# A four-layer graph network on one core: the adjacency handed over in three layouts, the transposed tile loaded and double-buffered

## The reference

```python
# layer 0: gated by the neighbours' keys
w = isqrt * mask * einsum('bid,bid->bi', q, einsum('bij,bjd->bid', adj, k * mask))
x += softmax(w, axis=1)[:, :, None] * v
# layer 1: attention weighted by adj, one head
weight = adj * exp(q @ k.T);  weight /= weight.sum(axis=2);  x += weight @ v
# layer 2: eight heads, scores multiplied by adj + adj
x += softmax(q @ k.T * scale * (adj + adj)) @ v @ Wo + bo
# layer 3: three-hop propagation
t = adj * exp(leaky_relu(sj[:, None, :] + si[:, :, None] + ab))
t /= t.sum(-1) + 1e-12
x += relu(h @ Wk[0] + (t @ h) @ Wk[1] + (t @ t @ h) @ Wk[2] + bk.sum(0))
```

## Time and profile before

| | |
|---|---|
| median of 3 runs | 2275.75 us (2275.45 to 2278.11) |
| profiled execution | 2281.91 us, span 2280.1 us |
| TensorE busy | 2246.0 us (99%), granted clock 0.995 |
| VectorE, ScalarE, GpSimd busy | 1314.0, 784.9, 717.8 us |
| DMA | 224.75 MB, 185048 packets, queue of SyncE 35.1% of 16 engines |

### The profile page before, as it was taken

One profiled execution on the slowest core, in us unless ns is written; L12 is line 12 of the kernel. 1 busy time (PEld: TensorE's weight loads), 2 busy tenths in 40 slices (PEclk: granted clock), 3 DMA queues, 4 the chain that ended last, 5 costly groups with the idle time before them and its releaser, 6 DMA issues.

```text
span 2280.1 us, 39533 instructions
## 1 busy us (share of the span) xinstructions
PE 2246.0 (99%) x15903; PEld 1779.9 (78%) x15903; DVE 1314.0 (58%) x2645; ACT 784.9 (34%) x1401; POOL 717.8 (31%) x926
## 2 busy tenths in 40 slices
PE   8999999999999999999999999999899999999998
PEld 5778888888888877888888888888677777777776
DVE  3565565565655665554656455665665757575752
ACT  3332332333322333233333333232343434343432
POOL 2343343334333423223332223332351313131320
PEclk9999999999999999999999999999899999999999
DMA  6223333333333343332333332333444343535341
GB/s 199 75 75 96 96 107 102 84 92 94 84 95 96 102 135 111 99 101 80 85 101 92 101 97 80 91 105 93 123 123 111 84 114 82 129 68 127 71 106 37
DMA packets 185048, 224.75 MB, mean 99 GB/s; under 512 B 68688, under 2 KB 85152, under 8 KB 184864
## 3 DMA queue, kind: packets, MB, share of 16 engines
q1 hardware_dynamic: 179104, 214.35, 35.1%
q10 hardware_dynamic: 5760, 7.87, 1.4%
HBM read 88.91 MB, written 50.37 MB: 61 GB/s over the span
## 4 chain that ended last, share of the span: by engine, by line
PE 90%; SPq 3%; DVE 3%; DMA 2%; ACT 1%; issue 1%; POOL 1%; DVEq 0%; ACTq 0%
PE bank L329 49%; PE bank L319 28%; PE bank L345 3%; PE bank L603 3%; SPq L1430 2%; PE bank L533 1%; PE bank L503 1%; PE bank L309 1%; PE bank L380 1%; DMA si<-stB 1%; PE bank L296 0%; DVE hs L668 0%; DMA arows<-stB 0%; DMA small<-in_L_gnn_ab 0%; ACT g1T L1037 0%
## 5 line engine op out<-in xcount | busy, mean ns | idle before, releaser
L329 PE MATMUL bank<-w_hi,h3T_hi 128*128 128x512 f32 x768 | 306.4, 399 | 1.8 <-ACT Z L988 1.8
L329 PE MATMUL bank<-w_lo,h3T_hi 128*128 128x512 f32 x768 | 300.3, 391 | 0.0
L329 PE MATMUL bank<-w_hi,h3T_lo 128*128 128x512 f32 x768 | 300.0, 391 | 0.0
L1235 POOL TENSOR_SCALAR stA<-stA 128x4 f32<-128x4 f32 x48 | 11.5, 239 | 682.8 <-DVE stA L645 682.7
L1002 ACT ACTIVATE hn<-x,stA 128x512 f32<-128x512 f32 x192 | 140.7, 804 | 233.9 <-POOL stA L1240 228.0
L643 DVE BATCH_NORM_STATS2 stA<-x 128x6 f32<-128x512 f32 x192 | 128.3, 668 | 149.2 <-DMA x<-mid 148.8
L329 PEld LDWEIGHTS bank<-w_hi,h3T_hi 128*128 128x128 f32 x768 | 144.7, 188 | 56.8 <-issue 25.2
L988 ACT ACTIVATE Z<-bank 64x512 f32<-64x512 f32 x256 | 151.7, 593 | 96.1 <-PE bank L329 78.8
L329 PEld LDWEIGHTS bank<-w_hi,h3T_lo 128*128 128x128 f32 x768 | 144.8, 188 | 30.6
L329 PEld LDWEIGHTS bank<-w_lo,h3T_hi 128*128 128x128 f32 x768 | 144.8, 189 | 29.0
L1248 POOL TENSOR_TENSOR h1T_lo<-hGB,h1T_hi 128x512 fp32r<-128x512 f32 x64 | 80.6, 1288 | 200.9 <-ACT h1T_hi L988 200.9
(11 more groups left out here) (217 smaller groups left out, 5720.8 us busy)
## 6 DMA issues: line engine op xcount, KB each, us to landing
hGA<-hs SPq DMA_DIRECT2D x768, 64.0 KB, 2.0
mid<-x SPq DMA_DIRECT2D x32, 1024.0 KB, 4.5
x<-mid SPq DMA_DIRECT2D x32, 1024.0 KB, 6.2
x<-in_x SPq DMA_DIRECT2D x16, 1024.0 KB, 5.9
hGB<-hs SPq DMA_DIRECT2D x256, 64.0 KB, 2.0
out<-x SPq DMA_DIRECT2D x15, 1024.0 KB, 9.5
blk<-in_adj SPq DMA_DIRECT2D x128, 64.0 KB
PT<-hs SPq DMA_DIRECT2D x120, 64.0 KB, 2.1
```

What stands on the lines that cost most here:

```text
L329: ins = eng.matmul(b[:], h[l][:, k, ts], W[r][:, k, :], start=(k == 0 and i == 0), stop=(last and k == 3 and i == 2))
```

## The change

The host hands the adjacency over three times, each in the order of its tile: `adj_rows` and `adj_cols` with 256 values per partition row, `adj_heads` with 512. VectorE's `adj_T` and its semaphore `v_at` are gone. SyncE loads the transposed tile by one DMA of 128 KB, into one of two buffers: the old `atc`, and the first 256 columns of `blk`. Since a load now goes straight to the tile that is read, it waits for the product of two groups before (`p_ex`, `p_al`); in layer 3 the buffer in `blk` also waits until `bo2` has been used. The load of `bo2` waits for `p_ex` of the last group in place of the last transpose. Layer 2's adjacency comes in two DMAs per group in place of four.

```diff
-        atc = alloc(root, "atc", [128, 4, 64])
+        adj_T = [alloc(root, "atc", [128, 256])[:], blk[:, 0:256]]
...
-            def adj_T(layer, g):
-                k = nT(layer, g)
-                dve.wait_ge(d_ab, 64 * k + 64)
-                dve.wait_ge(p_ex, min(k, NG))
-                dve.wait_ge(p_al, max(k - NG, 0))
-                eng.transpose(atc[:].rearrange("p t (r b) -> p t b r", b=2),
-                              blk[:, 32:544].rearrange("p (t b n) -> p t b n", t=4, b=2)[:, :, :, 0:32]).then_inc(v_at, 1)
...
-                    adj_T(0, g - 1)
...
-                        adj_T(3, 0)
...
-                    adj_T(3, g + 1)
...
                     pool.wait_ge(a_ex, 4 * g)
-                    pool.wait_ge(v_at, g)
-                    eng.tensor_tensor(ex[:], ex[:], atc[:], ALU.mult).then_inc(p_ex, 1)
+                    pool.wait_ge(*adj_T_loaded(nT(0, g - 1)))
+                    eng.tensor_tensor(ex[:], ex[:], t4(adj_T[nT(0, g - 1) % 2]), ALU.mult).then_inc(p_ex, 1)
...
-                pool.wait_ge(v_at, NG + g + 1)
+                pool.wait_ge(*adj_T_loaded(nT(3, g)))
...
-                eng.dma_start(abf[:, g % 2], adj_t[g]).then_inc(d_adj[g % 2], 16)
+                eng.dma_start(abf[:, g % 2].rearrange("p t n -> p (t n)"), adj_rows[g]).then_inc(d_adj[g % 2], 16)
...
                 k = nT(layer, g)
-                sp.wait_ge(v_at, k)
-                if layer == 3 and g == 0:
+                sp.wait_ge(p_ex, min(k - 1, NG))
+                sp.wait_ge(p_al, max(k - 1 - NG, 0))
+                if layer == 3 and k % 2:
                     sp.wait_ge(p_xb, 4 * NG)
-                for a in range(2):
-                    for bj in range(2):
-                        p0 = a * 64 + bj * 32
-                        eng.dma_start(blk[p0:p0 + 32, 32 - 32 * bj:544 - 32 * bj].rearrange("p (t n) -> p t n", t=4),
-                                      adj_b[g, a]).then_inc(d_ab, 16)
+                eng.dma_start(adj_T[k % 2], adj_cols[g]).then_inc(d_at[k % 2], 16)
...
-                    av = a2[g % 2][:].rearrange("p t (a n) -> p t a n", a=2)
-                    for h in range(2):
-                        for c in range(2):
-                            eng.dma_start(av[HALF[h], :, c, :], adj_v[g, c]).then_inc(d_adj[g % 2], 16)
+                    for h in HALF:
+                        eng.dma_start(a2[g % 2][h, :, :].rearrange("p t n -> p (t n)"), adj_heads[g]).then_inc(d_adj[g % 2], 16)
...
             sp.wait_ge(p_am, NG)
-            sp.wait_ge(v_at, NG)
+            sp.wait_ge(p_ex, NG)
             eng.dma_start(bv2, L2_gnn_bv.partition_broadcast(128)).then_inc(d_bv2, 16)
```

More of the change, by code:

```diff
@@ L72, in t4, with build @@
     return ap.rearrange("p (t n) -> p t n", t=4)
-def build(nc, x, adj, nodemask, L0_gnn_Wqk, L0_gnn_Wv, L1_gnn_Wq_w, L1_gnn_Wq_b, L1_gnn_Wk_w, L1_gnn_Wk_b,
+def build(nc, x, adj_rows, adj_cols, adj_heads, nodemask, L0_gnn_Wqk, L0_gnn_Wv, L1_gnn_Wq_w, L1_gnn_Wq_b, L1_gnn_Wk_w, L1_gnn_Wk_b,
           L1_gnn_Wv_w, L1_gnn_Wv_b, L2_gnn_Wq, L2_gnn_bq, L2_gnn_Wk, L2_gnn_bk, L2_gnn_Wv, L2_gnn_bv, L2_gnn_Wo,
@@ L84, in build @@
     mask_v = nodemask.rearrange("(g t a) n -> g a t n", g=NG, t=4)
-    adj_t = adj.rearrange("(g t a) i j -> g (a i) t j", g=NG, t=4)
-    adj_b = adj.rearrange("(g t a) (r b) j -> g a r t (b j)", g=NG, t=4, b=2)
-    adj_v = adj.rearrange("(g t a) i j -> g a i t j", g=NG, t=4)
     root = ExitStack()
@@ L112, in build @@
         d_adj = sems("adj_in0 adj_in1")
-        d_ab = sem("adj_blocks_in")
+        d_at = sems("adj_cols_in0 adj_cols_in1")
         d_mask = sem("mask_in")
@@ L130, in build @@
         d_h = sems("h_in0 h_in1 h_in2 h_in3")
-        (a_g0, a_g1, v_at, p_am, v_am, v_amr, v_ws, v_z, a_z, v_p, v_pcol) = sems(
-            "g0 g1 adjT am amS am_read ws zrow zexp prow pcol")
+        (a_g0, a_g1, p_am, v_am, v_amr, v_ws, v_z, a_z, v_p, v_pcol) = sems(
+            "g0 g1 am amS am_read ws zrow zexp prow pcol")
         (v_x1, v_dot, v_ec, v_vf, a_ex, p_ex, v_rc, v_x2) = sems(
@@ L273, in adj_loaded @@
         def adj_loaded(layer, g):
-            n, base = {0: (16, 0), 2: (64, NG // 2 * 16)}[layer]
+            n, base = {0: (16, 0), 2: (32, NG // 2 * 16)}[layer]
             return d_adj[g % 2], base + n * (g // 2 + 1)
@@ L279, in nT, with adj_T_loaded @@
             return (NG if layer == 3 else 0) + g
+        def adj_T_loaded(k):
+            return d_at[k % 2], 16 * (k // 2 + 1)
         hi_of = {n: 4 * i + 4 for i, n in enumerate(("m0", "v0", "a1", "v1", "q2", "k2", "v2", "o2", "w2", "w1", "w0"))}
@@ L1337, in l3_alpha @@
                 pool.wait_ge(a_ee, g + 1)
-                pool.wait_ge(v_at, NG + g + 1)
+                pool.wait_ge(*adj_T_loaded(nT(3, g)))
                 if g:
                     pool.wait_ge(*bank.done(("asum", g - 1)))
-                eng.tensor_tensor(al[:], ec3[:], atc[:], ALU.mult).then_inc(p_al, 1)
+                eng.tensor_tensor(al[:], ec3[:], t4(adj_T[nT(3, g) % 2]), ALU.mult).then_inc(p_al, 1)
             def l3_rowsum(g):
@@ L1623, in _ @@
             sp_program(eng)
-_INS = ["x", "adj", "nodemask", "L0_gnn_Wqk", "L0_gnn_Wv", "L1_gnn_Wq_w", "L1_gnn_Wq_b", "L1_gnn_Wk_w", "L1_gnn_Wk_b",
+_INS = ["x", "adj_rows", "adj_cols", "adj_heads", "nodemask", "L0_gnn_Wqk", "L0_gnn_Wv", "L1_gnn_Wq_w", "L1_gnn_Wq_b", "L1_gnn_Wk_w", "L1_gnn_Wk_b",
         "L1_gnn_Wv_w", "L1_gnn_Wv_b", "L2_gnn_Wq", "L2_gnn_bq", "L2_gnn_Wk", "L2_gnn_bk", "L2_gnn_Wv", "L2_gnn_bv",
         "L2_gnn_Wo", "L2_gnn_bo", "L3_gnn_Wv", "L3_gnn_bv", "L3_gnn_aw", "L3_gnn_ab", "L3_gnn_Wk", "L3_gnn_bk"]
+_ADJ = {"adj_rows": (0, 2, 3, 1, 4), "adj_cols": (0, 2, 4, 1, 3), "adj_heads": (0, 3, 1, 2, 4)}
 def kernel(**inputs):
@@ L1639 @@
     for name in _INS:
-        a = _np.ascontiguousarray(inputs[name])
+        a = inputs["adj" if name in _ADJ else name]
+        if name in _ADJ:
+            a = _np.transpose(_np.reshape(a, (NG, 4, 2, NN, NN)), _ADJ[name])
+            a = _np.reshape(a, (NG, -1, 4 * NN if name != "adj_heads" else 8 * NN))
+        a = _np.ascontiguousarray(a)
         arrays[f"in_{name}"] = a
```

## The result

The changed kernel takes 2282.04 us (2281.04 to 2284.80) and the kernel before, on the same chip, 2275.89 us (2274.74 to 2278.11), ten runs each: a ratio of 1.0024, 95% interval 1.0016 to 1.0033. It is slower by 6.1 us, where 2275.1 us, 0.6 us less, was forecast. The profiled execution took 2281.81 us, a span of 2280.0.

The account below looks back on a forecast made before the run. TensorE, busy 2246.0 of 2280.1 us, was taken as the bound; only joints between layers could matter. Terms 0 + 0 + 0.6 + 0 gave 0.6 us less than 2275.75, so 2275.1 us, range 2271.0 to 2278.5 (about 0.85).

Parts of the forecast that it names:

- the last sentence on DMA issues: Start and joint at 1640 us: no adjacency load precedes what TensorE waits for there, so fewer DMA issues change nothing, 0.
- only one has adjacency work in its chain: Of the joints between layers, only the layer 3 start has adjacency work ahead of TensorE; only there was time saved, 0.6 us.
- Rivals 4 and 5: Slower: bo2's late load delays layer 3, 2283.4 us, chance 0.03; or the single block load lands late, 2281.7 us, chance 0.02.
- rival 4: Third layer's output bias bo2 comes late, 7.6 us delay reaching TensorE at the joint, 2283.4 us; chance 0.03.
- The transposes at 0: VectorE's 32 block transposes, 14.2 us busy plus 25.8 us standing before them, hidden under TensorE's unbroken stream: worth 0.
- DMA issues and traffic in the middle at 0: Between the joints, 208 adjacency issues becoming 80 only lets SyncE's queue wait longer: worth 0.
- The queue and the rings in front of `si(1)`, 0.6 us: Layer 3 start: queue saves 0, less block traffic in the rings lands si of group 1 0.6 us sooner, bounds 0 to 3.0.
- the first term: SyncE's queue at the layer 3 start: si also waits for VectorE's sums, so fewer block issues save 0.2 us at most, taken as 0.
- The clock at the start of layer 3 at 0: TensorE's fall to half clock after the layer 3 gap probably still comes: 0, with a possible gain of 3.0 us.
- rival 1: Clock stays up after the smaller gap at the layer 3 start, or falls for half as long: 2272.2 to 2273.7 us; chance 0.20.
- `bo2` and `p_ex` at 0: End of layer 2's predecessor work: bo2's load waits for p_ex until 862.7 us, leaving 9.9 us of slack, so 0.
- the 0.04 for slower: Whole kernel: chance 0.04 of being slower by over 0.2%, above 2280.3 us.

Follow-up runs that it names:

- e13_first16: Changed kernel with only the write si(0) in 16-byte pieces, the fifteen others in four-byte pieces; ratio 0.9997 to the kernel before.
- e9_cols16: Kernel before with only the transposed tile's single load and double buffer, no VectorE transposes, and si written in 16-byte pieces; ratio 0.9970 to the kernel before.
- e10_loads16: Kernel before with only the new row and head loads, and si written in 16-byte pieces; ratio 0.9981 to the kernel before.
- e6_after16: Changed kernel with all si writes as 128 pieces of 16 bytes in place of 512 of four; 2273.04 us, ratio 0.9970 to the kernel before.
- e4_loads: Kernel before with only the new row and head loads, block loads and VectorE's transposes kept, four-byte si; ratio 1.0059 to the kernel before.
- e16_delay: Changed kernel with the four-byte write si(0) held until the last group's first ctx bank; ratio 0.9989 to the kernel before.
- e3_cols: Kernel before with only the transposed tile's single load and double buffer, no VectorE transposes, four-byte si; ratio 1.0040 to the kernel before.
- e14_rest16: Changed kernel with si(0) in four-byte pieces and the fifteen other si writes in 16-byte pieces; ratio 1.0001 to the kernel before.
- e7_twice: Changed kernel with the four-byte si writes made twice, the second to a tensor nobody reads; ratio 1.0597 to the kernel before.
- e12_beforetwice: Kernel before with the four-byte si writes made twice, the second to a tensor nobody reads; ratio 1.0604 to the kernel before unaltered.
- e1_null: Kernel before, unchanged, run and profiled again in a later session; ratio 1.0001 to itself, profiled span 2275.1 us.

## Why the prediction was wrong, point by point

**The step that failed** is the last sentence on DMA issues: "The start and the joint at 1640 us have no adjacency load in front of what TensorE waits for there ... 0." That is true of the waits in the trace of before, and the cost came from something that is no wait in that trace. With it fell the sentence that of the joints "only one has adjacency work in its chain", which had left this one out. In the changed kernel, while the four-byte write `si(0)` is outstanding, TensorE stands still for 3.34 us after 118 of 128 small products, waiting for no semaphore, and the lower clock it has there lasts longer. The missing term is 6.2 us by `e13_first16` (5.9 us in the chain of the joint). The writes had been named in the prediction as the longest piece of the next chain, but only as a latency for who waits for `si`; that they could hold up others was not among the rivals. Rivals 4 and 5, the two that had the kernel slower, named other causes, and neither came. (The 7.6 us of rival 4 should have read 7.2, from 862.7 - 855.45; nothing hangs on it.)

**The transposes at 0: right.** VectorE has 32 instructions less and is busy 1305.2 in place of 1314.0 us; no stretch of TensorE's stream moved. The 3.5 and 4.0 us waits at the joint were 4.3 and 4.0 in the first profile of before, 2.5 and 4.5 in the second.

**DMA issues and traffic in the middle at 0: right**, by the three long stretches and by `e9_cols16` and `e10_loads16`.

**The queue and the rings in front of `si(1)`, 0.6 us: the right sign.** The changed kernel's chain there:

```profile
1685.80 11.24 DMA si<-stB
```

The landing is 12.62 - 11.24 = 1.4 us faster than in the earlier trace rows, inside the bounds of 0 to 3.0, and the wait for `al` fell from 1.9 to 0.4 us. But the second profile of the unchanged kernel has 11.71 us for the same write and 0.9 us of wait for `al`, so at most 0.5 us of either belong to the change, and two profiles of one kernel differ by more (12.62 and 11.71). The write waited for VectorE's sums (1684.63 + 1.15 = 1685.78) and not for the block load, as the first term said.

**The clock at the start of layer 3 at 0: right for the change, and rival 1 right in part.** The clock fell again after the wait. Where the wait goes altogether (`e6_after16`), it stays up, and this place and the later groups together return 0.0020 to 0.0027. That the size of the gap decides, as rival 1 had it, is not borne out: between 1695 and 1720 us TensorE is idle for 2.19 us in the changed kernel with a granted clock of 0.93, and for 3.79 us in `e4_loads` and 2.78 in `e16_delay` with 1.00.

**`bo2` and `p_ex` at 0: right.** SyncE issues the load of `bo2` at 861.44, where 862.7 was worked out; between 850 and 920 us TensorE's waits are those of before (0.9 and 0.7 us), and rivals 4 and 5 did not come.

**Range and chances.** The range of 2271.0 to 2278.5 us and the 0.04 for slower held only named mechanisms, each with a place in the old chain. `e3_cols` and `e4_loads` show how much such a stall, with the waits in layer 3 that come with it, is worth in this kernel: 9 to 13 us. A range that allowed for it would have reached some 10 us up.

**What stays open.** That the small write makes the stall is shown: it goes when the write is made in larger pieces (`e6_after16`, `e13_first16`), when it is moved (`e16_delay`), and it stays when all others are changed but this one (`e14_rest16`). How it reaches TensorE is not. The first theory's way, a slow transfer of TensorE's instructions, is half borne out: beside the four-byte writes such packets are slow. In the packet records no execution has one over 2 us before 1600 us, where neither `arows` nor `si` is written; after it the kernels with all sixteen writes of `si` in four bytes have three to five (up to 5.4 us), those with all in 16 bytes none or one (2.55 and 3.00 us). But the rows speak against the slow packet as what TensorE waits for. In `e4_loads` TensorE stands still with no packet under way; in `e7_twice` the stall outlasts it by 9.4 us; in `e12_beforetwice` it takes 12.6 us with hardly a stall. And in `e1_null` the same packet, by its place in the row of 125, starts only at 1657.24, after TensorE has finished all 128 small and 12 large products at 1654.60: it was not needed for them. In the changed kernel and in `e14_rest16` stall and slow packet may have one cause in common. The Trainium skill (DMA: Bandwidth & Descriptors, Back-pressure in remote DMA) says of transfers between cores that stalled writes stall the other queues of the same DMA engine; the slow packets are compatible with it, for writes to DRAM, but no run separates the engines. Nor is it settled why the kernel before passes this joint unharmed with the same write at the same moment, or why either half of the change is enough to end that. No run varied one load at a time.

## What to carry to other kernels

A kernel with little waiting can still be moved by a quarter of a per cent by a change that saves work, if a burst of tiny DRAM writes lies near its joints; look for such writes first, and give them a price for the bystanders and not only for their reader. When a half of a change costs more than the whole, suspect a stall that comes and goes rather than the cost of an operation: move or reshape the one suspect event and see. And when two things are slow at once, look for a run that has one without the other before calling one the cause of the other. Here the same bytes in pieces four times as large are worth 0.2 to 0.3%, while the 128 DMA issues and 32 transposes that the change saved are worth nothing that can be measured.

## What the runs showed of the hardware

- 512 pieces of four bytes to DRAM, 2 KB in all, land 9.1 to 12.6 us after their issue; the same 2 KB in 128 pieces of 16 bytes land after 1.4 us. For `arows` it was 8.3 to 10.4 us (9.64 in the earlier trace rows) against 1.5.
- While the four-byte pieces of `si(0)` were outstanding, TensorE stood still among small products for 3.34 us (changed kernel), 4.33 (`e14_rest16`), 4.95 (`e4_loads`) and 12.30 (`e7_twice`, twice the pieces) with no semaphore to wait for; with 16-byte pieces it never did there.
- 16 KB packets of instructions took 4.3 and 3.9 us beside these writes, and 0.96 us when the writes came just after (`e16_delay`). In `e4_loads` the stall came without such a packet.
- A multiply with a running sum on VectorE, 128 x 512 in float32, takes 1265 ns with plain operands and 1664 ns with all operands in four runs of 128 and one of them read at a stride of 16 bytes.
- Two four-byte writes per group in place of one made either kernel 6% slower than the kernel before.
